# Router products of raw rows, a 16-byte record per token in layer 1, and expert rows gathered from HBM

## The reference, cut to what matters

```python
x = x + 0.5 * ffn(layernorm(x), w_router, w_gate, w_up, w_down)
x = x + attn(layernorm(x), W_proj, A, Bp, D, W_delta, b_delta)
x = x + 0.5 * ffn(layernorm(x), w_router, w_gate, w_up, w_down)

def ffn(x, w_router, w_gate, w_up, w_down):        # E = 32 experts, F = 256
    C = ceil(1.25 * T / E)                          # 640 places per expert
    probs = softmax(xt @ w_router); top1 = argmax(probs); gate = probs[top1]
    pos = cumsum(onehot(top1))[.., top1] - 1        # place in the expert's queue
    accepted = pos < C
    buf[top1 * C + pos] = xt                        # where accepted
    y = (silu(buf @ w_gate) * (buf @ w_up)) @ w_down
    return xt + where(accepted, y[slot] * gate, 0)

def attn(x, ...):                                   # per batch of 2048 tokens
    proj = x @ W_proj.T; delta, _, Cs, residual = split(proj, 4)
    delta = softplus(delta @ W_delta.T + b_delta)
    y = exp(delta*A)*B * sum(x*Cs) + cumsum(delta*B) * sum(Cs)
    return y + residual * D
```

## Time and profile before

| | us |
|---|---|
| median of 3 runs | 1674.33 (1673.36 to 1679.4) |
| the profiled execution: span from first to last instruction | 1587.6 |
| median of the runs less this span | 86.7 |
| PE / DVE / ACT / POOL busy | 1334.5 / 1265.9 / 1166.9 / 770.7 |
| indirect DMAs on POOL (L368; L850) | 256; 320 |

### The profile page before, as it was taken

The page is one execution under the profiler, slowest core; times in us unless marked ns, Lnnn a source line. Parts: engine busy times, 40 slices in busy tenths (PEclk is TensorE's granted clock), DMA queues, the critical chain, the costliest instruction groups (busy, mean ns, idle before and its releaser), DMA issues. The chain is left out here.

```text
span 1587.6 us, 31540 instructions
## 1 busy us (share of the span) xinstructions
PE 1334.5 (84%) x10174; PEld 1244.1 (78%) x10174; DVE 1265.9 (80%) x3493; ACT 1166.9 (74%) x2486; POOL 770.7 (49%) x917
## 2 busy tenths in 40 slices
PE   4546623999999999699999999997629999999997
PEld 3324413999999999599988898986619999999997
DVE  6576752999999999568899999998847877778775
ACT  6859923777777777479898898886647777777774
POOL 0067773344434444315557777876553434433443
PEclk8555555999999999899999999998859999999999
DMA  9999654667667667321222232211134444544541
GB/s 364 398 333 336 217 181 136 219 202 246 223 189 245 221 201 250 126 74 59 71 87 86 79 99 82 85 58 45 32 121 135 124 135 115 152 141 116 149 147 31
DMA packets 196882, 250.41 MB, mean 158 GB/s; under 512 B 24650, under 2 KB 182008, under 8 KB 192624
## 3 DMA queue, kind: packets, MB, share of 16 engines
q1 hardware_dynamic: 169072, 204.49, 40.5%
q0 software_dynamic: 27648, 43.91, 8.2%
HBM read 128.18 MB, written 152.47 MB: 177 GB/s over the span
## 5 line engine op out<-in xcount | busy, mean ns | idle before, releaser
L1041 PE MATMUL ps<-xs,ws 128*128 128x320 f32 x3072 | 465.5, 311 | 0.1
L1041 PEld LDWEIGHTS ps<-xs,ws 128*128 128x128 f32 x3072 | 455.5, 189 | 1.1 <-issue 1.1
L368 POOL DMA_INDIRECT slots<-xn,r x256 | 263.3, 1029 | 195.2 <-issue 76.4
L850 POOL DMA_INDIRECT x_rows<-ys,oidx x160 | 165.2, 1033 | 240.1 <-DVE ys L973 201.3
L850 POOL DMA_INDIRECT out<-ys,oidx x160 | 155.9, 975 | 246.8 <-DVE ys L962 184.2
L1041 PE MATMUL ps<-ws,hs 128*128 128x256 f32 x1920 | 262.0, 289 | 10.7 <-DVE ys L962 6.6
L1041 PEld LDWEIGHTS ps<-ws,hs 128*128 128x128 f32 x1920 | 239.0, 190 | 24.0 <-issue 22.3
L985 DVE TENSOR_TENSOR hf<-ps,sg 128x320 f32<-128x320 f32 x256 | 125.5, 490 | 85.7 <-ACT sg L904 84.6
L871 ACT CAST xs<-ps 128x512 fp32r<-128x512 f32 (+1 forms) x192 | 98.5, 513 | 129.7 <-PE ps L1034 129.7
L436 PE MATMUL ps<-cf,xn 128*128 128x128 f32 x512 | 110.7, 356 | 83.1 <-ACT xn L390 83.1
L925 DVE TENSOR_TENSOR ws<-wraw,ws 128x512 fp32r<-128x512 f32 x192 | 132.6, 692 | 58.2 <-ACT ws L864 55.5
(11 more groups left out here) (135 smaller groups left out, 2492.1 us busy)
## 6 DMA issues: line engine op xcount, KB each, us to landing
slots<-zero SPq DMA_DIRECT2D x32, 1300.0 KB, 9.3
xg<-slots SPq DMA_DIRECT2D x62, 650.0 KB
x_rows<-x SPq DMA_DIRECT2D x32, 516.0 KB, 9.3
x<-x_rows SPq DMA_DIRECT2D x32, 516.0 KB, 5.0
x<-in_x SPq DMA_DIRECT2D x32, 512.0 KB, 10.2
wraw<-in_w_gate SPq DMA_DIRECT2D x64, 256.0 KB
wraw<-in_w_up SPq DMA_DIRECT2D x64, 256.0 KB, 3.1
wraw<-in_w_down SPq DMA_DIRECT2D x64, 256.0 KB, 3.4
```

Of the source, the lines that this page charges most:

```text
L368: nc.gpsimd.indirect_dma_start(out=self.slots, out_offset=bass.IndirectOffsetOnAxis(ap=self.slot[:, t % self.xr, k:k + 1], axis=0), in_=se ...
L850: nc.gpsimd.indirect_dma_start(out=rows, out_offset=bass.IndirectOffsetOnAxis(ap=OIDX[:, e % YR, k:k + 1], axis=0), in_=YS[:, e % YR, k, : ...
L1041: ins = pe.matmul(dst, left(a, k), right(b, k), start=(n == 0), stop=(n == len(terms) - 1))
```

## The change

- **Router input.** TensorE transposes the raw rows of x; `act_norm`, the ring `xn` and the semaphores `rdone` and `normed` go. The mean is taken out of the router weights once at the start of `route` (`ONE`, two VectorE instructions), and `post` multiplies the shifted logits by 1/std (one more instruction of the size of L502). Scale factors are written to `META` in layer 1 and behind the row of x in layer 2.
- **Layer 1 scatters 16 bytes a token** into `table1`, which one small store blanks; the 16 fills of `slots1`, the wait for them and `GAP` go. The base rows are stored as before.
- **Experts of layer 1 gather rows.** GpSimd reads the token numbers of the table and gathers 128 rows of 1032 bytes per indirect DMA from `x1_rows`, three experts ahead (`AHEAD`) into a ring of five (`GR`). A place of the ring is free when the scatters of its former expert have landed (`y_out`). Layer 2 scatters rows that hold the base and the factors, as before by 128 indirect DMAs, and loads them from HBM with SyncE.
- **Experts normalize.** ScalarE's `x_norm` (five tiles, in place of `base`) works two experts ahead, and the output is added to the gathered row in place. `EMPTY`, `dve_empty`, `pe_total` and `out_index` go.
- **Attention's tail.** The router part stands two steps earlier (`BACK` 4, `LOGIT` 5, `POST_AT` from 13); the base of the last batch moves into the loop. The ring of x has 6 batches.

```diff
-XR, RR = 3, 4
+XR, RR = 6, 4
+GR = 5
+AHEAD = 3
...
-        slots1 = nc.dram_tensor("slots1", [DROP, RW], F32, kind="Internal").ap()
+        table1 = nc.dram_tensor("table1", [DROP, NF], F32, kind="Internal").ap()
...
                 pool.wait_ge(self.ready.sem, self.ready.at(c + 1))
+                if self.own:
+                    pool.wait_ge(self.based.sem, self.based.at(NC * t + lo // CH + u + 1))
                 apart(pool)
-                for k in tiles:
+                for k in (lo + 2 * u, lo + 2 * u + 1):
+                    i = TB * t + k
                     nc.gpsimd.indirect_dma_start(
-                        out=self.slots, out_offset=bass.IndirectOffsetOnAxis(ap=self.slot[:, t % self.xr, k:k + 1], axis=0),
-                        in_=self.xn[:, t % self.xr, k, :], in_offset=None, bounds_check=bound, oob_is_err=False,
-                    ).then_inc(self.scattered[t % self.xr], 16)
+                        out=self.places, out_offset=bass.IndirectOffsetOnAxis(ap=self.slot[:, i:i + 1], axis=0),
+                        in_=self.rows_of(i), in_offset=None, bounds_check=bound, oob_is_err=False,
+                    ).then_inc(self.scattered[t], 16)
...
             def pe_turn(self, pe, n):
-                pe.wait_ge(self.normed.sem, self.normed.at(n + 1))
                 pe.wait_ge(self.evac.sem, self.evac.at(n + 1 - len(self.bt)))
...
+                    dve.tensor_tensor(d, d, last(rb, E), ALU.mult).then_inc(self.chosen.sem, 1)
...
+        def first_meta(sp):
+
+            rows = table1.rearrange("(e p k) f -> p e (k f)", p=P, k=ET)
+            sp.dma_start(SLOT_META[:, 0:1], rows[:, 0:1]).then_inc(meta_in[0], 16)
+            sp.dma_start(SLOT_META[:, 1:E], rows[:, 1:E]).then_inc(meta_in[1], 16)
...
-                    for n in range(NFILL):
-                        fill(sp, 0, slots1, n)
-                        if n % 3 != 1 and 6 + n * 2 // 3 < 4 * XR:
-                            stream.load(sp, 6 + n * 2 // 3)
...
-                    pool.wait_ge(filled[0], 16 * NFILL)
-                    for S in range(SCATTER, NU + GAP + SCATTER + NC):
+                    pool.wait_ge(table_filled, 32)
+                    for S in range(SCATTER, NU + SCATTER + NC):
...
+                    def gather(e, k):
+                        if k == 0 and e == first:
+                            pool.wait_ge(meta_in[0], 16)
+                        if k == 0 and e == first + 1:
+                            pool.wait_ge(meta_in[1], 16)
+                        if e >= GR:
+                            pool.wait_ge(y_out[e % GR], 16 * ET * (e // GR))
+                        apart(pool)
+                        nc.gpsimd.indirect_dma_start(
+                            out=XG[:, e % GR, k, 0:HX], out_offset=None, in_=x1_rows, in_offset=place(e, k),
+                            bounds_check=last_row, oob_is_err=False,
+                        ).then_inc(xg_first[0] if e == first and k < 2 else xg_in[0][e % GR], 16)
...
+                    if turn == 0:
+                        last_row = pool.to_reg(T)
+                        for e in range(first, first + AHEAD):
+                            for k in range(ET):
+                                gather(e, k)
+                    for e in range(first, end + 1):
+                        for k in range(ET):
+                            if turn == 0 and e + AHEAD < end:
+                                gather(e + AHEAD, k)
+                            if e > first:
+                                scatter(e - 1, k)
...
-                    base(first)
+                    for q in range(NQ):
+                        x_norm(first + 1, q)
                     for e in range(first, end):
...
-                            base(e + 1)
+                        if e + 2 < end:
+                            for q in range(NQ):
+                                x_norm(e + 2, q)
...
-                TURN, DELTA, PLUS, RES, NORM, LOGIT = 0, 1, 2, 3, 6, 7
+                TURN, DELTA, PLUS, RES, BACK, LOGIT = 0, 1, 2, 3, 4, 5
...
-                COUNT_AT = [19 if t < BATCH - 2 else 17 for t, lo, hi in CHOICES]
+                COUNT_AT = [19 if t < BATCH - 2 else 17 if t < BATCH - 1 and hi < TB else 15 for t, lo, hi in CHOICES]
```

More of the change, by code:

```diff
@@ L152, in quarter, with factors, row @@
                 return self.X[:, (q + self.first) // 4 % XR, 4 * (q % 4):4 * (q % 4) + 4, 0:w]
+            def factors(self, t, tiles):
+                return self.X[:, (t + self.first // 4) % XR, tiles, HX:RW]
+            def row(self, k):
+                return self.X[:, (k + 4 * self.first) // TB % XR, k % TB, :]
             def moment(self, k, n, which):
@@ L495, in post @@
                 ct = ps[:, self.bc, 0:n * E].rearrange("p (e t) -> p e t", t=n)
[L496 to L497 removed]
+                mx, rr, se, gt, ci, acc, t1, t2, inv = (s[:, k, 0:n] for k in range(9))
+                row = self.factors(t, tiles)
+                rb, s1, hm = (v[:, t % RR, tiles] for v in (self.rb, self.s1, self.hm))
                 if step == 0:
@@ L681, in _ @@
                     nc.scalar.preload_act_table_set("natural_log_exp_and_others")
-                    for S in range(-2, NU + GAP + 22):
+                    for S in range(-2, NU + 22):
                         for g, (lo, hi) in enumerate(groups):
-                            if place(lo) + max(-3, 1 - lead[g]) == S:
+                            if lo + max(-3, 1 - lead[g]) == S:
                                 tail.act_rstd(act, g)
@@ L706, in _ @@
                     tail.dve_setup(dve)
-                    tail.rdone.grant(dve)
-                    for S in range(-2, NU + GAP + 22):
+                    tail.scaled.grant(dve)
+                    dve.memset(ONE[:], 1.0).then_inc(s_fresh, 1)
+                    for S in range(-2, NU + 22):
                         for q in (3, 2, 1, 0):
@@ L745, in _ @@
                     tail.pe_setup(pe)
-                    for S in range(NU + GAP + 22):
+                    pe.wait_ge(s_fresh, 2 * len(FRESH) + 1)
+                    for h in range(HC):
+                        ins = pe.matmul(ps[:, 4, 0:E], ONE[:], WR[:, h, :], start=(h == 0), stop=(h == HC - 1))
+                    ins.then_inc(s_prep, 1)
+                    for S in range(NU + 22):
                         if S == 4:
@@ L785, in macaron, with experts @@
         row_done = count("e_row_moments")
-        def experts(turn, slots, rows):
+        def experts(turn, rows):
             with ExitStack() as st:
@@ L855, in _, with place @@
-                    for e in range(first, end):
-                        scatter(e)
+                    def place(e, k):
+                        return bass.IndirectOffsetOnAxis(ap=factor(e, k, F_ID).bitcast(U32), axis=0)
+                    def gather(e, k):
[5 more added lines that the diff above has]
+                            pool.wait_ge(y_out[e % GR], 16 * ET * (e // GR))
+                        apart(pool)
+                        nc.gpsimd.indirect_dma_start(
+                            out=XG[:, e % GR, k, 0:HX], out_offset=None, in_=x1_rows, in_offset=place(e, k),
+                            bounds_check=last_row, oob_is_err=False,
+                        ).then_inc(xg_first[0] if e == first and k < 2 else xg_in[0][e % GR], 16)
@@ new lines, in scatter @@
+                    def scatter(e, k):
+                        if turn == 0:
+                            pool.wait_ge(row_done.sem, row_done.at(ET * e + k + 1))
+                        else:
+                            pool.wait_ge(ysum.sem, ysum.at(NQ * e + k // 2 + 1))
+                            if k >= 2 and e + 1 < end:
+                                pool.wait_ge(gu.sem, gu.at(4 * e + 4 + k - 1))
+                        apart(pool)
+                        nc.gpsimd.indirect_dma_start(
+                            out=rows, out_offset=place(e, k), in_=XG[:, e % GR, k, 0:width], in_offset=None,
+                            bounds_check=bound, oob_is_err=False,
+                        ).then_inc(y_out[e % GR], 16)
@@ L1164, in _ @@
                         stream.store(sp, q, tail.based)
-                        if q >= 1 and q - 1 + 4 * XR < NQ4:
-                            stream.load(sp, q - 1 + 4 * XR)
+                        ahead = q + 2 * XR
+                        if 4 * XR <= ahead < NQ4:
+                            if ahead % 4 == 0:
+                                sp.wait_ge(tail.scattered[ahead // 4 - XR], 16 * TB)
+                            stream.load(sp, ahead)
                     first_weights(sp, E)
@@ L1315, in _ @@
                                 a_norm(n)
-                    for n in range(NU - NC, NU):
-                        tail.act_base(act, n)
                 @block.vector
```

405 lines of the change are left out of this document (179 added, 226 removed).

## The result

The changed kernel takes 1786.9 us (median of 4 runs, 1784.4 to 1788.4), the kernel before 1673.95 beside it: 1.067 times as long (1.064 to 1.070), where I had forecast 1688.5, a ratio of 1.009. The direction was right, the size was not.

A forecast was written before the change was run, and what follows sets the result against it. Expert stages bound by TensorE, route and attention's end by POOL's scatter chains, with POOL's doubled list the worry in layer 1. Terms +22.6 (through layer 1) - 11.4 (attention) + 3.0 (layer 2's start) = +14.2 us, giving 1688.5; range 1648 to 1720.

The forecast's parts named there:

- I take this remainder as unchanged: Whole kernel: the runs' median of 1674.33 lies 86.7 us above the profiled span of 1587.6, and this stays.
- the third rival: Route: 16-byte row scatters take 0.3 us more than 1.30, so route ends 38 us later, 1727; chance 0.05.
- a cycle is 12.8 + 0.5 + 1.2 = 14.5: Layer 1, us per expert: ten indirect DMAs on POOL, VectorE's delays, landing wait; stage ends 22.6 us later.
- the landing wait: Layer 1: an expert's first gather waits for the scatter just ahead of it to land, 1.2 us a cycle.
- My upper bound of 16.3: Layer 1: longest cycle per expert in us, with the longest landing and 1.0 of delays.
- Rival 1: Layer 1: POOL turns around faster, cycle 12.8, -32 us, 1642; chance 0.30 for everything below 13.9.
- break-even: Layer 1: the cycle per expert at which the change neither gains nor loses time, put at 14.0 us.
- Rival 5: Layer 1: VectorE blocks POOL at every DMA, ten delays of 0.29 us, cycle +2.4, +65 us, 1754; chance 0.05.
- Rival 4: Layer 1: TensorE's clock falls in each expert's new wait; at 0.75 a 16 us cycle, +40, 1729; chance 0.04.
- 13.4 us earlier: Attention's tail: with the router steps moved forward, POOL's last chain of scatters ends at 1166.7 instead of 1180.1.
- of which I charge 2: Attention: VectorE gets some 6 us of added products; 2 us are charged to the time (bounds 0 and 6).
- Start of layer 2: Between the first rows' loads and the first products: five norms (2.6 us) now stand there, +3 us.

The follow-up runs named there:

- c9: Changed kernel as a mixture: layer 1 scatters whole rows again, 17 experts load their rows with SyncE, 15 gather; 1643.6 us.
- c5: Changed kernel with no edit, run on a quiet chip (one without late semaphore updates); 1682.4 us, 1.058 times the kernel before.
- c6: Changed kernel with a ring of six experts' rows in place of five (GR 6, AHEAD still 3); 1615.1 us.
- c8: Changed kernel without layer 1's gathers: SyncE loads rows of x in order, so experts compute on other tokens' rows; 1569.5 us.
- c4: Changed kernel with the lags of attention's tail as before (transposes at step 6, logits at 7); 1686.5 us.
- c11: Changed kernel with attention's product of shifted logits by 1/std replaced by a copy of 16 values; 1676.4 us.
- c10: Kernel with ring of seven and gathers four ahead, but three loads instead of five ahead of layer 2's barrier; 1603.9 us.
- c1: The kernel before with no edit, profiled again, on a quiet chip (no late semaphore updates); 1590.3 us, span 1588.5.
- c7: Changed kernel with a ring of seven and gathers four experts ahead (GR 7, AHEAD 4); 1602.1 us.

## Why the prediction was wrong

**The sum's base.** "I take this remainder as unchanged" failed as an account. It was not a remainder but time inside the span, on another kind of chip than the profiled one: 86 us there for the kernel before and 101 for the changed one, with late updates seen in both. In spans I was 79 us too low on a quiet chip (1681.1 - 1601.8), the misses below; the rest of the 98 (1786.9 - 1688.5) is mostly the 15 us by which a late chip costs the changed kernel more in these spans.

**Route** was right, on a quiet chip. First scatter 49.5 (I took 51), end 217.8 (217.3), first gather 221.8, first silu 239.5 (237.5), first scatter of layer 1 252.2 (251.3). A scatter of 16 bytes costs POOL what one of 1040 costs (0.99 us in the mean of either), so the third rival falls. c9 met the cost of short packets in another place: they burden the DMA engines, not POOL.

**Experts of layer 1** is the step that failed, though its mechanism stood: "a cycle is 12.8 + 0.5 + 1.2 = 14.5". It is 16.4, and the term that was mis-sized is the landing wait: 2.7 in place of 1.2. I had counted 2.3 us from the scatter's start and 0.2 for the release. From there to the release pass 3.2 at best (1.03 and 2.15 in the row of c5), 4.1 in the mean of the 16 waits, and 7 at the longest. The landing alone has a median of 2.9 in this stage; the 2.3 of the earlier trace rows is L368's, which stands in route and attention. Ten DMAs are 13.7, not 13.3, since each is 1.07 us busy, where the sum had 1.02 (0.97, and 0.5 for ten). My upper bound of 16.3 was built from the longest landing of those rows, and the mean cycle passes it. 27 x 1.9 = 51 us, and 4 more at the stage's end.

Rival 1 (12.8) falls; c6 shows that without the wait even 13.7 is the floor, and break-even was 14.0 only with attention's gain, which didn't come.

Rival 5 falls as well, and my reading that VectorE is what delays POOL's DMAs isn't borne out. The kernel before in the same stage (300 to 600 us):

```profile
L850 POOL DMA_INDIRECT x_rows<-ys,oidx x123 | 127.1, 1033 | 173.4 <-DVE ys L973 143.1 <-issue 29.4 <-PE ps L1041 0.6
```

That is 1.03 us in the mean with VectorE 95% busy; the changed kernel has 1.07 there with VectorE 68% busy, and 0.98 in layer 2 with 77%. The growth is 0.04 and not 0.29, and what makes it isn't shown.

Rival 4: the clock in this stage fell to 0.91 with TensorE 81% busy; c8, with TensorE busy for 296 of 300 us, has 1.00. With POOL's list accounting for the whole cycle, the lower clock adds nothing to it.

**Attention**: forecast -11.4, measured +3.7. "13.4 us earlier" measured some 3 (c4): the stretch from the last row's update to the last scatter did shrink by 5, but the steps moved forward land in a loop where VectorE is 85% busy, and part of it is lost there. "of which I charge 2" measured some 4 (c11): where an engine paces the loop, its added work counts nearly in full. VectorE's mix (L1412, L1404 before) rose from 500 to 539 ns a time, 5 us in all, with no change to it; with the old lags it is 506 (c4), so the rise comes with the moved steps.

**Start of layer 2**: +3 forecast, +11.5 measured. 6.4 us are the longer end of the block (c10), which the sum put at nothing, as if the new kernel's end were like the old one's. From there to the first silu pass 3.8 us more, most of it the norms as forecast, and 1.3 are in the rest of the stage.

## What to carry over

Where an engine's list runs in order, a wait for the landing of the entry just ahead of it costs the whole time to the release in that very stage (4.1 us here), not the median landing of other stages (2.3), and one more place in the ring takes it away (67 us here). Work moved onto an engine's list is free only up to what that engine has left: POOL had 5.6 us an expert (12.1 less five DMAs of 1.3) and got 6.9 and a wait. And if a profile's span and the median of the runs differ by 5%, as here, where on one chip they differ by 1.8 us, the two may come from different conditions; that is to be cleared up before any sum is made.

## What the runs showed of the hardware

- Chips differ by 5% for the same kernel (1590 and 1677), and one of the slower ones gave 1660 as well. There semaphore updates came up to 12.5 us after their instruction had ended (the rows above): in route and layer 1 of both kernels, less in attention (32 of 379 us of such waits in the changed kernel, 21 of 84 in the kernel before), not in layer 2, though it scatters too.
- From the start of an indirect scatter to the release of the gather that waits for its landing: 3.2 us in the row of c5, some 7 at the longest (6.0 of waiting behind 1.0 of the scatter). The median landing of a scatter was 2.1 us in layer 2 (1300 to 1600 us, 135 GB/s moved), 3.0 in layer 1 (300 to 600 us, 161 GB/s), 4.3 there in c8 (221 GB/s), but 2.5 in attention (950 to 1250 us, 71 GB/s). The Trainium skill (DMA: Bandwidth & Descriptors, "Latency and other measured facts") says that the fixed cost of a DMA grows with the load on HBM, whose access it gives as 0.2 us on average and 2 at high load; of these four figures three follow that direction and attention's does not.
- 9,600 fills of 16 bytes pulled the DMA throughput from 20 to 80 us to 292 GB/s, where the kernel before has 408, and to 61 from 16 to 32 us (c9). The Trainium skill (DMA: Bandwidth & Descriptors, "Specifications") says that transfers below 512 bytes are done by read-modify-write; no trace here shows the mechanism, only that they are dear for the DMA engines, while POOL's own time for short rows did not change (0.99 us in route with either).
- POOL's mean time per indirect DMA was 1.03 us in layer 1's experts before, 1.07 after, and 0.98 in layer 2. The Trainium skill (SBUF — State Buffer, "SBUF: two separate sides") says that VectorE can lock GpSimd out of a shared port; by VectorE's busy share alone (95, 68 and 77%) the three figures can't be ordered, and no run here shows such a lock.
- At the end of attention GpSimd's DRAIN ended 2.1 us after its last scatter in the kernel before (c1) and 9.2 in the changed one (c5, c10), where the next block's first instruction follows 0.25 us behind it.

No run beats the kernel before with the right output. The best of the changed design is c7, 1602 us, 0.7% slower; c8 says what its gathers cost.
